# Two attention stages of a decoder: query-first scores issued two slots ahead, row maxima transposed in the last slot, and a key tile's weighting and sums issued together every second slot

## The reference

```python
scores = jnp.einsum('bhqd,bhkd->bhqk', q, k) * scale
attn = jax.nn.softmax(scores, axis=-1)          # cross attention: causal mask before it
out = jnp.einsum('bhqk,bhkd->bhqd', attn, v)
```

## Time and profile before

| | us |
|---|---|
| median of 3 runs | 3028.73 (3028.34 to 3034.42) |
| span of the profiled execution | 3028.2 (its own device time is not listed apart; the two lower runs lie 0.1 and 0.5 above the span) |
| TensorE busy | 2476.7 (82%) |
| VectorE, ScalarE, GpSimd busy | 1884.0 (62%), 1239.5 (41%), 851.9 (28%) |
| layer-0 attention, from first scores to last | 66 to 640 of the span |
| second attention function | 1576 to 2450 of the span |

### The profile page before, as it was taken

How to read it: one execution, slowest core, us unless ns; L and a number is a source line. 1 busy time by engine, 2 the same in 40 slices (tenths; PEclk the granted TensorE clock), 3 DMA queues, 4 the chain that set the end, 5 groups by cost and what they waited for, 6 DMA issues and landing times. The chain is left out here.

```text
span 3028.2 us, 35090 instructions
## 1 busy us (share of the span) xinstructions
PE 2476.7 (82%) x12822; PEld 1644.7 (54%) x12822; DVE 1884.0 (62%) x2959; ACT 1239.5 (41%) x1873; POOL 851.9 (28%) x1176
## 2 busy tenths in 40 slices
PE   5898989864443357999448999999999879999999
PEld 4454545321222237998334554545555538888887
DVE  3766575627899985778557777565655444444443
ACT  2444444428656625666103433334333323333332
POOL 2232222215657634555343332001211110000000
PEclk8999999976665678999768999999999979999999
DMA  3213132212222346988585655334433423101000
GB/s 117 65 43 84 43 84 46 70 61 77 77 80 77 108 163 213 308 300 289 158 185 136 159 146 157 88 89 104 109 95 91 115 80 127 42 0 42 1 28 15
DMA packets 186940, 323.55 MB, mean 107 GB/s; under 512 B 20450, under 2 KB 52066, under 8 KB 186788
## 3 DMA queue, kind: packets, MB, share of 16 engines
q1 hardware_dynamic: 168356, 270.44, 30.0%
q0 software_dynamic: 15360, 50.34, 6.3%
q10 hardware_dynamic: 3072, 0.79, 0.1%
HBM read 182.30 MB, written 62.92 MB: 81 GB/s over the span
## 5 line engine op out<-in xcount | busy, mean ns | idle before, releaser
L757 DVE TENSOR_REDUCE at_negmax<-at_ps 128x2 f32<-128x1024 f32 (+3 forms) x256 | 259.1, 1016 | 120.3 <-PE at_ps L523 63.1
L670 ACT ACTIVATE at_probs<-at_ps 128x1024 f32<-128x1024 f32 (+3 forms) x256 | 221.7, 866 | 267.4 <-PE at_ps L538 263.3
L1367 DVE TENSOR_REDUCE a_negmax<-a_ps 128x2 f32<-128x1024 f32 x128 | 155.2, 1217 | 136.4 <-PE a_ps L1120 135.8
L59 PE MATMUL ff_ps<-ff_xnT_hi,ff_s_hi 128*128 128x512 f32 x512 | 200.8, 392 | 5.1 <-DVE ff_xnT_lo L2878 5.1
L60 PE MATMUL ff_ps<-ff_xnT_lo,ff_s_hi 128*128 128x512 f32 x512 | 200.1, 391 | 0.0
L61 PE MATMUL ff_ps<-ff_xnT_hi,ff_s_lo 128*128 128x512 f32 x512 | 200.1, 391 | 0.0
L1946 ACT ACTIVATE gr_act_signs<-gr_signed,gr_test 128x512 bf16<-128x512 f32 x248 | 177.4, 717 | 42.3 <-POOL gr_test L2339 20.4
L2908 DVE TENSOR_TENSOR ff_hid<-ff_hid,ff_ps 128x512 f32<-128x512 f32 x64 | 44.0, 688 | 238.6 <-ACT ff_hid L2853 238.6
L538 PE MATMUL at_ps<-at_qk 98*128 98x512 f32 (+3 forms) x512 | 171.7, 417 | 21.0 <-DMA at_qk<-at_mrow 10.6
L1268 ACT ACTIVATE a_probs<-a_ps 128x1024 f32<-128x1024 f32 x128 | 130.8, 1023 | 135.2 <-PE a_ps L1138 134.6
L518 PE MATMUL at_ps<-at_qk 96*128 96x512 f32 (+3 forms) x512 | 162.9, 382 | 19.0 <-DVE at_xnT_lo L818 8.9
(11 more groups left out here) (431 smaller groups left out, 6640.1 us busy)
## 6 DMA issues: line engine op xcount, KB each, us to landing
at_qk<-at_part SPq DMA_DIRECT2D x384, 128.0 KB
first_gu<-in_L_ffn_w_gate_up_dram SPq DMA_DIRECT2D x32, 1024.0 KB, 13.4
a_qk<-a_part SPq DMA_DIRECT2D x192, 128.0 KB
first_d<-in_L_ffn_w_down_dram SPq DMA_DIRECT2D x32, 512.0 KB, 13.6
out_rows<-ex_y SPq DMA_DIRECT2D x32, 512.0 KB
gr_aside_raw<-in_L_ffn_W_dram SPq DMA_DIRECT2D x48, 256.0 KB, 3.1
w13T<-gr_aside_out SPq DMA_DIRECT2D x32, 256.0 KB, 3.2
shared_x<-x_after_cross SPq DMA_DIRECT2D x8, 1024.0 KB
```

The source lines that it names most:

```text
L59: pe.matmul(out, lh, rh, start=start, stop=False, skip_group_check=True)
L670: act.activation(probs[:, t % 2, 2 * w:2 * w + 2, lo:S], banks(("kq", g, s), lo), ACT.Exp, scale=SCALE).then_inc(free(("kq", g, s)), 1)
L757: dve.reduce_max(negmax[:, g % 2, :].rearrange("p (j t) -> p j t", t=NT)[:, 2 * w:2 * w + 2, t], banks(("qk", g, s), 0, width(g, t)), AX.X ...
L1367: dve.reduce_max(negmax[:, g % 2, :].rearrange("p (j t) -> p j t", t=NT)[:, 2 * w:2 * w + 2, t], banks(("qk", g, s)), AX.X, negate=True).t ...
```

## The change: what it does

In both functions:

- Query-first scores run two slots ahead of before: slot s of step g issues (g+1, s+2), and slots 6 and 7 issue (g+2, 0) and (g+2, 1). In `attention_linear` this holds with exceptions, since the projections come in twos: even steps g > 0 issue (g+1, s+2) in slots 0 to 5 and none in 6 and 7; odd steps issue (g+1, s) in slots 0 to 5, two units in slot 6 and (g+2, 0), (g+2, 1) in slot 7.
- The transposition of the maxima moves from the step's end into slot 7, behind the scores. In odd steps of `attention_linear` it moves into the first projection, after two of its four contraction chunks.
- The halves no longer stand one in each slot: both halves of a key tile are issued together in slots 1, 3, 5, 7 (`HALVES_AT`). ScalarE copies the weighted values in slot 1 instead of 0.
- `attention_linear`: the four output tiles stand in slots 1, 3, 5, 7 of step 4k+1.

```diff
@@ attention_layers
+        LEAD, MAXIMA_AT, HALVES_AT = 2, PAIRS - 1, {1: (-1, 6), 3: (0, 0), 5: (0, 2), 7: (0, 4)}
+
+        def score_units(g, s):
+            at = PAIRS * (g + 1) + s + LEAD
+            units = range(LEAD + 1) if (g, s) == (-1, 0) else (at,) if g >= -1 else ()
+            return [(n // PAIRS, n % PAIRS) for n in units if has(n // PAIRS)]
...
-                if has(g + 1):
-                    place("qk", g + 1, s)
+                for unit_of in score_units(g, s):
+                    place("qk", *unit_of)
+                if s == MAXIMA_AT and has(g + 1):
+                    place("mx", g + 1)
...
-                    if has(g + 1):
-                        scores_qk(g + 1, s)
-                    if s >= 2 and has(g):
-                        half(g, s - 2)
-                    if s < 2 and has(g - 1):
-                        half(g - 1, PAIRS - 2 + s)
+                    for unit_of in score_units(g, s):
+                        scores_qk(*unit_of)
+                    if s == MAXIMA_AT and has(g + 1):
+                        turn_maxima(g + 1)
+                    if s in HALVES_AT and has(g + HALVES_AT[s][0]):
+                        back, n = HALVES_AT[s]
+                        half(g + back, n)
+                        half(g + back, n + 1)
...
-                if has(g + 1):
-                    turn_maxima(g + 1)
...
-                    if s == 0 and has(g - 1):
+                    if s == 1 and has(g - 1):
...
-                if has(g + 1):
-                    maxima_rows(g + 1)
+                    if s == MAXIMA_AT and has(g + 1):
+                        maxima_rows(g + 1)
...
-                    if has(g + 1):
-                        maxima(g + 1, s)
+                    for unit_of in score_units(g, s):
+                        maxima(*unit_of)
...
@@ attention_linear
-        OUT_AT = {(0, PAIRS): 0, (1, 1): 1, (1, 3): 2, (1, 5): 3}
+        OUT_AT = {(1, 1): 0, (1, 3): 1, (1, 5): 2, (1, 7): 3}
+        LEAD, MAXIMA_AT, HALVES_AT = 2, PAIRS - 1, {1: (-1, 6), 3: (0, 0), 5: (0, 2), 7: (0, 4)}
...
+        def score_units(g, s):
+            if g % 2 == 0:
+                ahead = LEAD if g > 0 else 0
+                units = [(g + 1, s + ahead)] if s + ahead < PAIRS else []
+            elif s < PAIRS - LEAD or g < 0:
+                units = [(g + 1, s)]
+            elif s == PAIRS - LEAD:
+                units = [(g + 1, s + n) for n in range(LEAD)]
+            else:
+                units = [(g + 2, n) for n in range(LEAD)]
+            return [u for u in units if has(u[0])]
...
-            def project(g):
+            def project(g, between=None):
...
+                        if between is not None and (i, dc) == (0, 2):
+                            turn_maxima(between)
...
+                if g % 2 and has(g + 3):
+                    project(g + 3, g + 1 if has(g + 1) else None)
+                    project(g + 4)
+                elif g % 2 and has(g + 1):
                     turn_maxima(g + 1)
-                if g % 2 and has(g + 3):
-                    project(g + 3)
-                    project(g + 4)
```

More of the change, by code:

```diff
@@ L379, in attention_layers @@
                     place("w", weight(g, s))
-            if has(g + 1):
-                place("mx", g + 1)
             if has(g + 3):
@@ L1008, in attention_linear @@
                     place("kq", g, s)
-                if has(g + 1):
-                    place("qk", g + 1, s)
+                for unit_of in score_units(g, s):
+                    place("qk", *unit_of)
+                if g % 2 == 0 and s == MAXIMA_AT and has(g + 1):
+                    place("mx", g + 1)
                 if linear_unit(g, s, 2) is not None:
@@ L1021, in attention_linear @@
                     place("xT", turn_unit(g, s), 1)
-            if has(g + 1):
+            if g % 2 and has(g + 1):
                 place("mx", g + 1)
```

## The result

The changed kernel takes 3080.73 us (median of 4 runs, 3075.89 to 3098.24) against 3030.36 of the kernel before (4 runs): ratio 1.0169, 95% interval 1.0139 to 1.0200. It is slower, as forecast, but by 51 us instead of 9, and outside the range of 3008 to 3062. The profiled execution has a span of 3080.3 us at a mean granted clock of 0.893.

The account below looks back on a forecast made before the run. TensorE's own order of work was taken to bound both stages. From 3028.2, the second function's 4 + 14 - 22 - 4 + 11 + 1 = +4, then layer 0's +19 and -12.5, gave 3038.7, taken as 3038; range 3008 to 3062.

Parts of the forecast that it names:

- first pairs: Second function, slots behind a projection: second key-first scores wait for its banks; +0.51 full-width, +0.35 causal, +14 in all.
- Halves together: Second function, later full-width pairs: fourth scores wait for ScalarE's exponential, so a pair takes 4.39 against 4.28; +4 in all.
- Maxima in slot 7: Second function: TensorE's 26.1 us of waits before transposing the maxima go, less about 0.5 in 7 steps; net -22.
- tail: Second function: two steps without a following projection lose the 3.13 wait for row DMAs, fewer switches in the last; -4.
- The stack: Second function, slot 6: scores need the stack's 12 DMAs earlier; steps 4 and 8 pay 4 + 3, clock 4; +11.
- Rival 3: Stack late in all 8 batch-beginning steps and layer 0's odd steps, restarting at half clock; 3062, chance 0.20.
- my own case: Whole kernel: the summed terms hold, likeliest at 3028 to 3048 us, forecast 3038; chance 0.28.
- Layer 0, odd steps: Seven steps: two more score pairs, a longer wait at the memory and units meeting reductions, 2.7 each; +19.
- the memory's wait: Layer 0, odd steps, slot 3: waiting for ScalarE's copy of features, 0.92 today, grows by about 1.0.
- the four query-first units: Layer 0, odd steps, slots 6 and 7: they meet reductions of 1.217 us each; the last waits about 0.7.
- Layer 0, even steps: Output tile leaves the end of steps 4, 8, 12 (-4.5), two units leave others (-4), further steps -4; -12.5.

Follow-up runs that it names:

- x3: Second function only, against the kernel before: halves joined in slots 1, 3, 5, 7, lead and maxima as before; 3043.93 us, ratio 1.0041.
- x4: Second function only, against the kernel before: query-first scores two slots ahead and maxima in slot 7, single halves; 3042.58 us, ratio 1.0028.
- y4: Layer 0 only, against the kernel before: lead and moved maxima, single halves, outputs in their old slots; 3030.93 us, ratio 1.0004.
- w1: Second function's lead and maxima, single halves, two score units held from each fourth step's end to the next slots 0 and 1; against the kernel before 3022.85 us, 0.9973.
- x2: The whole change in attention_linear alone, attention_layers as in the kernel before; 3049.76 us, ratio 1.0060 against that kernel.
- y3: Layer 0 only, against the kernel before: lead, moved maxima and outputs' later slots, single halves; 3047.67 us, ratio 1.0049.

## Why the prediction was wrong

No single term holds the 42 us between 3038 and 3080.73. By pairs of slots the second function's +35.0 is +8.3 in the first pairs (I had +14), +22.2 in the two middle pairs (+4, with a share for the last) and +4.5 in the last, where the projection stands (-22 - 4 + 11 + 1 = -14). Layer 0 is +21.7 for 19 - 12.5 = +6.5.

**Halves together (+4) and first pair (+14): the mechanism right, the middle pairs mis-sized.** The plain pair is 4.36 for 4.39. The first pair was +0.42 for 0.51 (full-width) and +0.24 for 0.35 (causal). What I had at nothing are the other middle pairs: slots 4 and 5 behind a values unit (+0.54), and those of the causal steps, which I set at 0 and where one or both lose 0.44 to 0.66 in nearly every step. In x3, the halves alone, the middle pairs lose 17.2. Its sum of +14.1 (12 by the runs) is near my +18 by luck, since the last pairs gain 11.0 that I had not either.

**Maxima in slot 7 (-22) and tail (-4): the direction right, the size too large.** The wait fell from 26.9 to 7.8, but a removed wait is no removed time: the last pairs other than those of steps 0, 4 and 8 gain 13.2 in the changed kernel and 18.2 in x4. Why not more was not taken apart; in the changed kernel the joined halves take part of the same wait themselves (x3 has 19.3 of the 26.9 left).

**The stack (+11): the mechanism right, its places and size wrong.** I named it in steps 4 and 8, and got the stall of step 4 (4 us; 4.5 measured) from the point where the engines run dry. The last pairs of steps 0, 4 and 8 are 5.2, 6.1 and 6.35 longer, where the plain ones of steps 2, 6 and 7 are 0.5 shorter: 19 us for +11. Step 0, which I left out, waits 3.6. In step 8, which I took to stall less than step 4 (3 for 4), the stack needed 17.6 us from its first issue and the wait was 5.1. And the scores and halves behind these waits run at 1.2 GHz: the three pairs lose 6 beyond the waits' own 13.1, where I added 4 for two. Rival 3 (3062) was nearer than my own case, in part by luck: it had the stack stall all 8 steps that begin a batch, and it stalled three of them by 3.6 to 5.1 and two more by 0.7 and 1.2.

**Layer 0, odd steps (+19): two terms mis-sized.** I said +1.0 for the memory's wait; it grew by 0.7, as read. What I left out is the half clock that can follow it: +3.6 in the pair, in steps 7 and 11, but +0.4 in step 3. Slots 6 and 7, with the four query-first units, cost 2.0 for my 0.7; y4, with single halves, still has 1.5 of it. Steps 3, 7, 11 came to +17.4 for 8.1 forecast.

**Layer 0, even steps (-12.5): the gain came and was given back in the next step.** The query-first scores after step 8 do start 5.4 earlier in the step (415.29 - 391.95 = 23.3; before 408.34 - 379.58 = 28.8), as I took from the stack (5.2); the earlier trace rows are of steps 8 and 9, not 4 and 5. But the output tile was cover as well as load. With it gone the maxima's rows (2.94), which I had called hidden by the stack, and the stack (2.67) are waited for bare, and the step restarts at the low clock. The pairs of steps 4, 8, 12 and 5, 9, 13 sum to +15.9, for -4.5 + 8.1 = +3.6 forecast. Steps 14 and 15 saved 9.8, more than the 2 that I gave them.

The Trainium skill, "TensorE: Matmul & The Clock Gate", section HAM oscillation, says that gaps between bursts bring the clock down again. The trace agrees at the waits of 1.63, 1.86 and 2.3 to 6.4 us shown above, not at every one (last section). In the prediction I cited this rule and let it price one term; it had to stand beside every new wait, as a chance. By rows, a half behind a wait that it follows takes 1.94 instead of 1.06.

## What to carry to other kernels

Before taking an instruction out of a place where nothing waits, ask what its time covers: here a half of 1.00 us in front of the memory, an output tile of 3.7 us in front of a DMA. Bound the price of a new idle gap of TensorE by its length on one side, and by its length plus the next microseconds' work at half clock on the other: the same wait at the memory cost 0.4 us in one step and 3.6 in another, and which step pays changes from one trace to the next. When a transfer is needed earlier, take its landing time from a row of the same stage with the same traffic, and hold back only the units that it stops: the lead alone lost 0.28%, and the lead with two units held over the stack won 0.27%.

## What the runs showed of the hardware

The unexpected part is what follows a gap. Behind the memory's wait of 0.92 us TensorE ran on at 2.4 GHz. It ran at 1.2 GHz behind waits of 1.63 us (memory, steps 7 and 11), 1.86 us (banks, w1) and 2.3 to 6.4 us (stack). In layer 0 it worked without a gap at a granted clock of 0.50 to 0.56 from 356 to 362 before that rose. But the same 1.63 in step 3 of the same trace (1.00 granted from 203 to 209) and the 1.98 in w1's step 9 were followed by full clock, and in x2 it was step 3 that lost its clock and steps 7 and 11 that kept it. The 2.94 before step 9's first scores (0.73 at 411.89) and the 2.84 before y3's projection (0.47 at 461.17) were followed by full speed at first. So the length of the one wait doesn't tell it; what does was not tested. For the stack, twelve 128 KB transfers landed 9.4 us after the first issue in layer 0 (405.88 to 415.29, changed kernel) and 17.6 us after it beside the gathers and a 1 MB load. Issuing the twelve took 7.7 and 9.8 us; the median from issue to landing of one was 2.3 and 8.9.
